# Moving low parts between engines and letting ScalarE write the last rows: a mixture-of-experts kernel on one Trainium2 core

## The reference, cut to what matters

```python
h = einsum('bsi,bio->bso', x, W[id]) + b[id]          # x: (4, 256, 256); 4 of 16 conditioning matrices
def swiglu(x, w1, w2, w3): return silu(x @ w1) * (x @ w3) @ w2
xf = h.reshape(1024, 256)
y  = swiglu(xf, sw1, sw2, sw3)                        # shared expert, width 352
weights, indices = top_k(softmax(xf @ gate_w), 2)     # 8 experts, two of them per token
for e in range(8):                                    # routed experts, width 176
    y += cw[:, e:e+1] * swiglu(xf, rw1[e], rw2[e], rw3[e])   # cw: the weight where e was chosen, else 0
return x + y.reshape(4, 256, 256)
```

## Time and profile before

| | |
|---|---|
| median of 3 runs | 113.98 us |
| the profiled execution, its own time | 113.78 us |
| its span (first to last instruction) | 112.2 us |
| PE, DVE, ACT, POOL busy | 102.0, 67.1, 51.2, 46.8 us |
| granted TensorE clock, mean | 0.995 of full speed |
| chain that ended last | PE 57%, DMA 11%, DVE 10%, issue 8%, POOL 7% |

### The profile page before, as it was taken

One profiled execution on the slowest core, in us unless ns is written; L12 is line 12 of the kernel. 1 busy time (PEld: TensorE's weight loads), 2 busy tenths in 40 slices (PEclk: granted clock), 3 DMA queues, 4 the chain that ended last, 5 costly groups with the idle time before them and its releaser, 6 DMA issues.

```text
span 112.2 us, 2182 instructions
## 1 busy us (share of the span) xinstructions
PE 102.0 (91%) x604; PEld 86.4 (77%) x604; DVE 67.1 (60%) x221; ACT 51.2 (46%) x129; POOL 46.8 (42%) x61
## 2 busy tenths in 40 slices
PE   6997997897599996999999999999999999999780
PEld 4786886674488864677889998999999997988540
DVE  1324673717999955578877775565745643121991
ACT  4045575589092422466655754455565555100000
POOL 5280078763677900005653345334534535710000
PEclk9999999999999999999999999999999999999997
DMA  1897999997987016554232424232021110009955
GB/s 45 260 335 240 357 353 354 378 391 220 301 243 265 32 58 209 162 134 114 95 134 73 146 81 126 104 119 64 5 75 60 53 68 25 0 11 343 379 202 187
DMA packets 16736, 19.07 MB, mean 170 GB/s; under 512 B 2338, under 2 KB 13718, under 8 KB 16726
## 3 DMA queue, kind: packets, MB, share of 16 engines
q1 hardware_dynamic: 13302, 12.62, 35.6%
q0 software_dynamic: 1984, 4.46, 11.0%
q10 hardware_dynamic: 1440, 1.86, 4.8%
HBM read 12.64 MB, written 7.21 MB: 177 GB/s over the span
## 4 chain that ended last, share of the span: by engine, by line
PE 57%; DMA 11%; DVE 10%; issue 8%; POOL 7%; another core or an unknown queue 3%; ACT 1%; POOLq 0%; DVEq 0%; SPq 0%; ACTq 0%
PE bank L846 36%; POOL rows_by_expert L392 6%; PE bank L978 5%; PE bank L1013 4%; DVE x_area L806 4%; DMA rows_by_expert<-h_area,slot 4%; PE bank L858 4%; DMA y_area<-_out_by_choice_and_token 3%; PE bank L833 3%; DMA h_area<-rows_by_expert 2%; DMA _out_by_choice_and_token<-y_area,dest 2%; PE bank L840 2%; DVE hT_area L548 2%; PE bank L873 1%
## 5 line engine op out<-in xcount | busy, mean ns | idle before, releaser
L408 POOL DMA_INDIRECT _out_by_choice_and_token<-y_area,dest x23 | 23.5, 1021 | 35.8 <-DVE y_area L762 24.1
L392 POOL DMA_INDIRECT rows_by_expert<-h_area,slot x16 | 17.9, 1117 | 12.4 <-DVE slot L625 8.2
L846 PE MATMUL bank<-w_all,hsT_hi 128*128 x72 | 21.6, 342 | 0.0
L846 PE MATMUL bank<-hT_area,sh_area 128*128 128x512 f32 (+1 forms) x72 | 17.4, 396 | 1.9 <-DVE sh_area L543 1.9
L846 PEld LDWEIGHTS bank<-hT_area,sh_area 128*128 128x128 f32 (+1 forms) x72 | 12.7, 179 | 5.9 <-DVE sh_area L543 2.4
L846 PEld LDWEIGHTS bank<-w_all,hsT_hi 128*128 128x128 f32 x72 | 13.0, 188 | 0.0
L756 DVE TENSOR_TENSOR y_area<-y_area,bank 128x176 f32<-128x176 f32 x23 | 7.7, 336 | 8.8 <-ACT y_area L503 4.6
L503 ACT ACTIVATE y_area<-bank 128x176 f32<-128x176 f32 x23 | 7.3, 318 | 9.7 <-PE bank L846 7.6
L543 DVE TENSOR_TENSOR hsT_lo<-bank,hsT_hi 128x256 fp32r<-128x256 f32 x18 | 7.6, 424 | 6.9 <-ACT hsT_hi L499 5.7
L846 PE MATMUL bank<-w_all,hsT_lo 128*128 x36 | 11.5, 320 | 0.0
L846 PE MATMUL bank<-raw,gT_f 88*128 x44 | 11.3, 378 | 0.0
(11 more groups left out here) (128 smaller groups left out, 192.1 us busy)
## 6 DMA issues: line engine op xcount, KB each, us to landing
h_area<-rows_by_expert SPq DMA_DIRECT2D x23, 128.0 KB, 2.0
raw<-in_L_ffn_rw_dram SPq DMA_DIRECT2D x16, 176.0 KB
raw<-in_L_ffn_rw_dram SPq DMA_DIRECT2D x2, 704.0 KB
rows_by_expert<-x_area SPq DMA_DIRECT2D x8, 128.0 KB
y_area<-_out_by_choice_and_token SPq DMA_DIRECT2D x4, 256.0 KB, 4.6
y_area<-_out_by_choice_and_token ACTq DMA_DIRECT2D x4, 256.0 KB, 5.2
out_dram<-x_area SPq DMA_DIRECT2D x3, 256.0 KB, 2.0
sh_raw<-in_L_ffn_sw_dram SPq DMA_DIRECT2D x2, 352.0 KB, 3.8
```

Source lines behind the costliest of these rows:

```text
L392: nc.gpsimd.indirect_dma_start(out=rows_dram, out_offset=bass.IndirectOffsetOnAxis(ap=slot[:, i, t:t + 1], axis=0), in_=h_sb[:, t, :], in_ ...
L408: nc.gpsimd.indirect_dma_start(out=y_dram, out_offset=bass.IndirectOffsetOnAxis(ap=dest[:, j:j + 1], axis=0), in_=y_sb[j % NBY], in_offset ...
L846: last = nc.tensor.matmul(dst, w, v, start=start and n == 0, stop=stop and n == len(operands) - 1)
```

## The change

1. POOL now makes the low part of shared column block 1 as well: two scatters of batch 0, `sh_lo(0)`, two scatters, `sh_lo(1)`, then the other batches. DVE keeps block 2 alone.
2. On DVE the first two `w13_lo_of` move from ahead of `shared_gate(3)` to behind `shared_gate(5)`, where now all four stand in a row.
3. At the end three token halves instead of two are weighed on PE: (2,0), (2,1) and (3,1). x itself is added in PSUM too, as a product with the identity. ACT instead of DVE copies these three from PSUM to `x_area`, and ACT's queue writes the very last half. Half (3,0) stays with DVE. Two more diagonals are made in the loop.

```diff
-        diagonal = [[sb(f"diagonal{b}{i}", [P, P]) for i in range(TOPK)] for b in range(B - BH)]
+        late_units = [(b, j) for b in range(BH, B) for j in range(JS) if (b, j) != (B - 1, 0)]
...
@@ sync
-            for b in range(B - 1):
+            for b in range(BH):
                 sp.wait_ge(out_ready, JS * (b + 1))
                 sp.dma_start(out_tiled[b], x_sb[:, b].rearrange("p j d -> p (j d)")).then_inc(out_stored, 16)
-            for j in range(JS):
-                sp.wait_ge(out_ready, JS * (B - 1) + j + 1)
-                sp.dma_start(out_tiled[B - 1][:, j * D:(j + 1) * D], x_sb[:, B - 1, j, :]).then_inc(out_stored, 16)
+            for b in range(BH, B - 1):
+                sp.wait_ge(late_out_ready, JS * (b - BH + 1))
+                sp.dma_start(out_tiled[b], x_sb[:, b].rearrange("p j d -> p (j d)")).then_inc(out_stored, 16)
+            sp.wait_ge(out_ready, JS * BH + 1)
+            sp.dma_start(out_tiled[B - 1][:, 0:D], x_sb[:, B - 1, 0, :]).then_inc(out_stored, 16)
...
@@ gpsimd
-            dispatch(0)
-            pool.wait_ge(sh_hi_ready, 1)
-            nc.gpsimd.tensor_tensor(sh_lo[:, :, shared_cols(0)], sh_raw[:, :, shared_cols(0)],
-                                    sh_hi[:, :, shared_cols(0)].bitcast(F32), ALU.subtract).then_inc(sh_lo_pool, 1)
+            def sh_lo_of(c):
+                cols = shared_cols(c)
+                pool.wait_ge(sh_hi_ready, c + 1)
+                nc.gpsimd.tensor_tensor(sh_lo[:, :, cols], sh_raw[:, :, cols], sh_hi[:, :, cols].bitcast(F32),
+                                        ALU.subtract).then_inc(sh_lo_pool, 1)
+
+            dispatch(0, [0])
+            sh_lo_of(0)
+            dispatch(0, [1])
+            sh_lo_of(1)
             for b in range(1, B):
                 dispatch(b)
...
@@ scalar
             read_rows(act, 1)
+            for n, (b, j) in enumerate(late_units):
+                act.wait_ge(weighed_ready, n + 1)
+                nc.scalar.copy(x_sb[:, b, j, :], y_acc[b][j]).then_inc(late_out_ready, 1)
+            act.wait_ge(late_out_ready, len(late_units))
+            act.dma_start(out_tiled[B - 1][:, D:2 * D], x_sb[:, B - 1, 1, :]).then_inc(out_stored, 16)
...
@@ vector
-            sh_lo_of(1)
             shared_gate(0)
...
-            w13_lo_of(0)
-            w13_lo_of(1)
             shared_gate(3)
             shared_gate(4)
             shared_gate(5)
-            w13_lo_of(2)
-            w13_lo_of(3)
+            for e in range(E // 2):
+                w13_lo_of(e)
...
-                base_of(B - 1 - b, 0, 2 * JS + 1 + b)
-
-            for b in range(BH, B):
-                dve.wait_ge(y_in[b], 16 * TOPK)
-                dve.wait_ge(base_ready, JS + 3)
-                for i in range(TOPK):
-                    weigh(b, i, 0)
-                dve.wait_ge(weighed_ready, b - BH + 1)
-                nc.vector.tensor_tensor(x_sb[:, b, 1, :], y_acc[b][1], x_sb[:, b, 1, :], ALU.add).then_inc(out_ready, 1)
+            dve.wait_ge(y_in[B - 1], 16 * TOPK)
+            for i in range(TOPK):
+                weigh(B - 1, i, 0)
...
@@ tensor
-                add_products(y_acc[b][j], [(gated[0:shared_rows(c), c, toks], sh2_raw[0:shared_rows(c), c, :])
-                                           for c in range(NSH)], True, b < BH or j == 0).then_inc(acc_ready, 1)
+                products = [(gated[0:shared_rows(c), c, toks], sh2_raw[0:shared_rows(c), c, :]) for c in range(NSH)]
+                if (b, j) in late_units:
+                    products.append((ident[:, :], x_sb[:, b, j, :]))
+                add_products(y_acc[b][j], products, True, (b, j) not in late_units).then_inc(acc_ready, 1)
...
-            for b in range(BH, B):
+            for b, j in late_units:
                 pe.wait_ge(y_in[b], 16 * TOPK)
-                add_products(y_acc[b][1], [(diagonal[b - BH][i][:, :], y_tok[:, b, i, D:2 * D]) for i in range(TOPK)],
+                add_products(y_acc[b][j], [(diagonal[b, j][i][:, :], y_tok[:, b, i, j * D:(j + 1) * D]) for i in range(TOPK)],
                              False, True).then_inc(weighed_ready, 1)
```

36 lines of the change are left out of this document (20 added, 16 removed).

## The result

In the first comparison the changed kernel took **117.69 us** (median of 4 runs, 116.61 to 119.74) against 114.05 (113.71 to 114.43) before: ratio 1.0235 (95% interval 1.0187 to 1.0283). The forecast was 112.7, the range ended at 114.2. The profiled execution took 116.61 us, with a span of 115.0. A ratio compares only the executions of each kernel that lie close to its fastest ones, and so it can differ from the quotient of two medians.

A forecast was written before the change was run, and what follows sets the result against it. Until 43 us the chain through POOL's scatters was taken as the bound, then PE without gaps. From 113.78 us, -1.53 (freed scatter) and +0.25 (end) gave 112.5; the median lies 0.2 above: 112.7 us, range 111.7 to 114.2.

The forecast's parts named there:

- the unnamed wait of 3.04 us at 22.73: On DVE, in the chain before the changed places; POOL's different traffic could move it by some tenths either way.
- outside all of this: Where the prediction put DVE's unexplained 3.04 us wait: not among its cases or their chances.
- Part 1: Second shared low part on POOL: costs 1.33 us there, covered by 2.29 us of idle time, so nothing on the chain.
- cover gone, it would cost up to 1.3: POOL's idle time before the last eight scatters missing: the low part moved to POOL would cost up to 1.3 us.
- Part 2: w13 subtractions behind the gates free the last scatter, 0.98 instead of 3.19 us: 2.21 gained, 1.53 after one new overlap.
- One meeting: Third of the eight scatters falls under sh_lo_of(2) on DVE and ends 0.68 us late, leaving 1.53 us gained; 33%.
- the 0.02 us: at_tile expected 0.24 us into the seventh scatter, where 0.22 was a hit and 0.26 a miss.
- two meetings: Rival: the seventh scatter is also hit, by at_tile, losing another 0.67 us; 0.86 gained, 113.4 us; 18%.
- Part 3: At the end, weighing three token halves on PE makes PE late: 0.2 to 0.25 us slower, bounds 0 and 0.6.
- The sum: Whole kernel, profiled execution: -1.53 + 0.25 = -1.28 us, giving 112.5, and 112.7 for the median.
- within 1%: Whole kernel: outcome not told from no change, since a measurement can tell about 1%, 1.14 us; chance 0.46.
- taken as it is: Landing behind the last scatter, assumed unchanged at 1.43 us behind its end.
- PE goes cold: Rival: before the loop, PE idle 2 to 3 us drops to half clock; 115.4 to 118 us; 8%.

The follow-up runs named there:

- e1_pool: Only the second shared low part moved from DVE to POOL, against the kernel before: 115.33 us, ratio 1.0144.
- e11_pool_again: Only the second shared low part moved from DVE to POOL, against the kernel before, measured again: 115.13 us, ratio 1.0101.
- e13_pool_third: Only the second shared low part moved from DVE to POOL, against the kernel before, a third time: 115.30 us, ratio 1.0092.
- e8_one_input: Kernel before, with the two w13 low parts ahead of the gates replaced by a one-input operation of the same output: 114.28 us in one run.
- a4_after: The changed kernel, no edit, in a fourth session against the kernel before: 116.93 us, ratio 1.0218.
- e9: Kernel before with all w13 low parts behind the gates, at_tile behind the fifth gate product, eight warming products before the row transposes: 114.71 us, ratio 0.9983.
- a2_after: The changed kernel, no edit, measured again for a second profile, against the kernel before: 113.85 us, ratio 0.9992.
- a3_after: The changed kernel, no edit, measured once more against the kernel before: 113.92 us, ratio 0.9964.
- b2_before: The kernel before, no edit, measured again for a second profile: 114.40 us, ratio 0.9983.
- e2_gates: Only the two routed w13 low parts moved behind the last shared gate product, against the kernel before: 113.84 us, ratio 0.9826.

## Why the prediction failed, step by step

- **The step that failed: the unnamed wait of 3.04 us at 22.73, put "outside all of this", at "some tenths either way".** It was late counts, and they do two things to the prediction. In the first comparison they held PE for 3.73 us, with 1.6 us of half clock behind it, so that the loop started 1.90 us later instead of 1.5 earlier (last item). And the slack that paid for part 1 came from them.
- **Part 1, "the chain doesn't move": wrong.** It rested on 2.29 us of POOL's slack before 27.05, which that wait had made. In the profiles without late counts the slots come at 22 to 23 us, and POOL goes from batch 1 straight to the eight, which start 1.2 us later: the case "cover gone, it would cost up to 1.3", which I had named and not priced. At the last scatter 0.65 of it is left, since the subtraction that DVE no longer makes had held two scatters. e1_pool, e11_pool_again and e13_pool_third show the loss by itself.
- **Part 2, -1.53: right in its mechanism, and in size.** The long scatter goes (3.25 to 1.64), which gives 1.6. One meeting of that size remains, but under `at_tile` and not under `sh_lo_of(2)`: that the size was met is in part luck. That an operation with *two* SBUF inputs is needed was wrong (e8_one_input), and that a scatter is open to it only in its first 0.1 to 0.2 us too: `at_tile` begins 0.27 us into the scatter at 32.28 and holds it, where 0.26 at 28.31 was a miss. All nineteen profiles together: every scatter to `rows_by_expert` that took 1.1 us or more ended 0.83 to 0.85 us behind a DVE operation. `at_tile`, begun 0.21 to 0.28 into a scatter, held it in fourteen profiles of fourteen; `sh_area`, begun 0.12 to 0.26 into one, held it in none of four (before, after, a4_after, e9, the profiles with late counts; but `at_tile` held in before too). So the place in the scatter alone doesn't decide it, and the 0.02 us on which I weighed the rival "two meetings" told nothing. One difference is that `at_tile` follows at once on a row of `at_row` operations; nothing tested that. The Trainium skill ("SBUF — State Buffer", section "SBUF: two separate sides") has a DVE operation with two SBUF inputs and a GpSimd operation that reads SBUF lock a shared port pair against each other: whichever starts first has it for its whole instruction. It counts DVE operations in a two-port mode among them too, which float32 copies and `tensor_scalar` can enter. The 2.51 us of e8_one_input agree with the latter. With "whichever starts first" the trace does not agree: the scatter at 32.28 had begun 0.27 before `at_tile` and was the one to wait.
- **Part 3, +0.25: right in sign, nearly in size.** In a2_after PE's diagonal products start without a wait and ACT's last copy ends 14.2 us behind the shared products' start (14.4 in a3_after), against 14.3 forecast. The span's end is at 16.57 behind it, against 16.09 in b2_before: 0.3 to 0.5 us lost. The further half a microsecond in the first session lies in the landing of the copies, which comes late in some kernels with the end as before too.
- **The sum without late counts**: -1.60 + 0.65 + 0.3 to 0.5 is -0.45 to -0.65, so 113.4 against a median of 113.98. Measured: -0.1 and -0.4, with intervals of 0.7 to 0.9 us to each side. With the cover priced, the forecast would have been "within 1%". The landing behind the last scatter, "taken as it is" at 1.43, is not fixed either: SP's first load of rows stands 1.65 us behind the last scatter in before and in a2_after, and up to 4.76 (e2_gates) where the scatters end earlier.
- **The rival "PE goes cold" (8%)** had the right mechanism. Its place, before the loop, was wrong for the first comparison: there PE stood still for 3.73 us among the shared products, and 1.6 us of the loss is the clock behind it. Without late counts the clock does fall before the loop, but more often in the kernel before (33 of 35 runs) than in the changed one (6 of 12), so that it works for the change. The profile that the prediction was read from, with its clock at full until 111 us, was the exception. For the "2 to 4" microseconds at that level no row was given; the runs show 3.41 or 6.83 at 0.50, and 1.1 to 2.7 us more for the loop.
- **What made it 117.7** was none of my cases: late counts, in which PE stood still for 3.7 to 6.5 us in the shared experts. That the counts were late is shown by the trace. That it is a state of the session is shown by four sessions of the same kernel. The kernel before pays for it too, about 1 us: at full clock it takes 114.1 us in a4_after's session (8 runs) and 113.0 in the sessions without late counts (8 runs). It gets that back because its clock holds in 8 of 17 runs there, and in 8 of 89 in the others, so its median stays. Why the changed kernel pays 3 us is argued from four profiles, by POOL's pause, and not shown. What makes the counts late is open.

## What to carry to other kernels

A slack in one profile is only as good as the wait that makes it: when the wait ahead of it has no name, take a second execution before spending it, or price the edit at both ends. Long operations on VectorE that have all tiles in SBUF are best kept away from the indirect DMAs of GpSimd, and that move alone (with PE kept busy through its gap) was the best version here with a narrow interval, 0.9889. When a repeat differs by more than its interval, compare the same waits in both profiles before explaining either.

## What the hardware did that I had not expected

- Counts of semaphores arrived up to 10.7 us after the product that raised them (27.68 and 38.34), in two of seven sessions, while indirect DMAs were under way; in a2_after 0.02 us after.
- A float32 operation with one SBUF input (0.47 us for 128x704) held a scatter as one with two (0.84) did: it ended 0.84 us behind the last of them. But `sh_area` subtractions that began 0.12 to 0.26 into a scatter held none of four.
- PE at 1.2 GHz for 3.41 us behind idle gaps of 1.03 and 1.69 us in one profile (b2_before), and not behind one of 1.90 in another (a2_after): 1.2 to 1.7 us of the whole.
- The profiles with late counts lack records of semaphores (1750 to 1795 arrivals in all, against some 2600 in the others), so a missing arrival is no proof of a late one.
- POOL's subtraction of 128x512 float32 took 1.29 to 1.31 us, near the 1.33 worked out from 128x384; DVE's takes 0.67 to 0.68.
